# Eight rows of attention and a mixture of experts on one core: first slot reordered, two late rows' scores two a head, gathers ahead of the finishing operations

## What is computed

```python
ct_q = _lin(x, w_down_q, b_down_q)
q = (_lin(ct_q, w_up_q, b_up_q) + _rope(_lin(ct_q, wq_r, bq_r), cos, sin)).reshape(bs, sl, nh, hd)
ct_kv = _lin(x, w_down_kv, b_down_kv)
k = (k_ct + rope_k).reshape(bs, sl, nh, hd)
probs = softmax(einsum('bqhd,bkhd->bhqk', q, k) / sqrt(hd))
a = einsum('bhqk,bkhd->bqhd', probs, v).reshape(bs, sl, nh * hd)
x = x + _layernorm(_lin(a, wo, bo))
...
routed = einsum('etf,efh->eth', up * silu(gate), down_proj)   # one expert a token, times its score
shared = silu(x @ shared_gate_w) * (x @ shared_up_w) @ shared_down_w
x = x + _layernorm(shared + routed.sum(0))
```

## Time and profile before

| what | us |
|---|---|
| median of 3 timed runs (433.12 to 434.48) | 433.74 |
| the profiled execution's own time | 429.76 |
| its span, first to last instruction | 427.9 |
| TensorE busy | 397.9 (93%) |
| VectorE busy | 273.4 (64%) |
| ScalarE busy | 208.1 (49%) |
| GpSimd busy | 129.6 (30%) |
| head 0 of slot 0 on TensorE | starts at 33.48 |
| head 0 of slots 5, 6, 7 | 154.2, 178.65, 199.92 |
| last matmul ends, last VectorE instruction ends | 417.4, 425.3 |

### The profile page before, as it was taken

One profiled execution on the slowest core, in us unless ns is written; L12 is line 12 of the kernel. 1 busy time (PEld: TensorE's weight loads), 2 busy tenths in 40 slices (PEclk: granted clock), 3 DMA queues, 4 the chain that ended last, 5 costly groups with the idle time before them and its releaser, 6 DMA issues.

```text
span 427.9 us, 9422 instructions
## 1 busy us (share of the span) xinstructions
PE 397.9 (93%) x3383; PEld 299.3 (70%) x3383; DVE 273.4 (64%) x629; ACT 208.1 (49%) x383; POOL 129.6 (30%) x184
## 2 busy tenths in 40 slices
PE   7998789999999999797989999999999999999990
PEld 6675456676776767374668999999994444589990
DVE  5674478787879786877475594222225898727775
ACT  1644647676675858555561112444446766311110
POOL 1423412516253434303211101212212220026872
PEclk9999899999999999899999999999999999999997
DMA  8899326364553736460127660011111111123422
GB/s 263 204 116 122 62 70 194 87 175 136 153 156 89 216 96 209 100 199 1 52 98 230 223 215 25 26 51 51 50 51 44 44 45 35 51 59 104 141 95 86
DMA packets 50756, 47.29 MB, mean 111 GB/s; under 512 B 5334, under 2 KB 45526, under 8 KB 50710
## 3 DMA queue, kind: packets, MB, share of 16 engines
q1 hardware_dynamic: 44779, 38.31, 34.2%
q0 software_dynamic: 1632, 4.46, 3.6%
q10 hardware_dynamic: 4299, 3.92, 2.7%
HBM read 25.19 MB, written 8.65 MB: 79 GB/s over the span
## 4 chain that ended last, share of the span: by engine, by line
PE 79%; DVE 8%; DMA 4%; issue 3%; ACT 3%; POOL 2%; ACTq 0%; DVEq 0%; POOLq 0%
PE bank L1388 40%; PE bank L1707 7%; PE bank L1392 6%; PE bank L1576 6%; PE bank L1556 5%; PE bank L1517 5%; PE bank L1732 3%; DMA stacks<-mT 2%; PE bank L1455 2%; DVE nmax L1057 2%; PE bank L1445 2%; PE bank L1503 1%; DVE wall L1087 1%; DVE stats_at L991 1%; POOL rstd_at L641 1%
## 5 line engine op out<-in xcount | busy, mean ns | idle before, releaser
L1057 DVE TENSOR_REDUCE nmax<-bank 128x2 f32<-128x512 f32 x112 | 74.4, 686 | 26.4 <-PE bank L1517 25.6
L1388 PEld LDWEIGHTS bank<-stacks,wall 128*128 128x128 f32 x512 | 59.8, 192 | 2.5 <-issue 1.9
L1388 PE MATMUL bank<-stacks,wall 128*128 128x128 f32 x512 | 61.2, 276 | 0.4 <-ACT stacks L909 0.4
L1263 DVE TENSOR_TENSOR stacks<-stacks,bank 128x512 f32<-128x512 f32 x34 | 23.3, 687 | 51.7 <-PE bank L1388 49.1
L873 ACT ACTIVATE pv<-bank 128x512 f32<-128x512 f32 x64 | 38.3, 603 | 36.7 <-PE bank L1576 35.8
L1576 PE MATMUL bank<-stacks 99*128 99x256 bf16 x256 | 49.5, 276 | 3.8 <-DMA stacks<-mT 3.3
L873 ACT ACTIVATE wall<-bank 128x512 f32<-128x512 f32 x64 | 38.5, 606 | 27.2 <-PE bank L1576 26.2
L909 ACT ACTIVATE stacks<-bank 128x512 f32<-128x512 f32 x34 | 20.3, 597 | 64.3 <-PE bank L1388 54.3
L1517 PE MATMUL bank<-stacks 96*128 96x256 bf16 x224 | 43.2, 278 | 6.4 <-DVE nmax L1057 6.2
L1388 PE MATMUL bank<-wall,stacks 128*128 128x256 f32 (+1 forms) x208 | 49.2, 380 | 0.0
L706 POOL DMA_INDIRECT stacks<-x_sc,row_i x18 | 19.9, 1105 | 89.5 <-PE bank L1392 70.5
(11 more groups left out here) (207 smaller groups left out, 795.4 us busy)
## 6 DMA issues: line engine op xcount, KB each, us to landing
stacks<-low_sb SPq DMA_DIRECT2D x144, 64.0 KB, 2.5
wall<-gate_up SPq DMA_DIRECT2D x8, 1024.0 KB, 5.4
wall<-down SPq DMA_DIRECT2D x8, 512.0 KB, 6.9
y_exp<-stacks ACTq DMA_DIRECT2D x18, 128.0 KB, 1.7
x_tok<-wall SPq DMA_DIRECT2D x8, 256.0 KB, 2.5
stacks<-x_tok SPq DMA_DIRECT2D x16, 128.0 KB, 2.5
out<-stacks SPq DMA_DIRECT2D x8, 256.0 KB, 2.1
stacks<-low_sb SPq DMA_DIRECT2D x12, 128.0 KB, 5.9
```

Source lines behind the costliest of these rows:

```text
L1057: dve.tensor_reduce(nmax[:, half, qt, 2 * pair:2 * pair + 2], two(sm_bank[u % 2]), AX.X, ALU.max, negate=True).then_inc(sm["sm_max"], 1)
L1263: dve.tensor_tensor(to, sg, fu[:, :], ALU.mult).then_inc(sm["h_sb"], 1)
L1388: last = pe.matmul(out_ap, lhsT, rhs, start=(n == 0), stop=(n == len(pairs) - 1))
```

## The change

- Slot 0: unit 15 of row 0 and the down projection of row 2 come before head 0 instead of behind it. GpSimd splits the second half of the maxima of row 0 at head 0 (head 5 before), TensorE turns and ScalarE sends them at head 3 (head 5 before). The key and query copies of row 2 come at head 4, and the two query copies of row 2 move from ScalarE to VectorE (`third_q`). The units of row 1 run two a head from head 8 on (one head earlier than before), M0 of row 1 a head earlier. The first half of row 0's maxima is sent by SyncE in both versions.
- Before slot 0: 12 more matmuls of ones, and 8 each behind the first turn and the first down projection of row 0.
- Slots 5 and 6 follow a second table `late` on each engine, and `UNITS_AT` puts the units of rows 6 and 7 at one or two a head, so that the last is at head 10 and head 11. The projection `D_wo` moves from head 10 to 9, the division steps, N_v, D_aT a head earlier, the router a head earlier, M0 from head 12 or 13 to 9 and 10 (7 on GpSimd), and GpSimd splits the second half of the maxima in the same slot behind `D_power`. The turn of row 4 or 5 (`E_xn2T`) keeps its head, 3 of slot 6 and 2 of slot 7.
- First expert tiles: the turn of tile 9 (`X:9`) comes before the gate and up products of tile 8 (`GR:8`), its copy before a silu.
- Finishing operations: three pairs of gathers come before the finals, pair c + 3 after the power of final c. The first tile of pair 6 is added before the work of tile LAST - 1, into a buffer of its own, the first of pair 7 before LAST.

```diff
-WARM_ONES = 54
+WARM_ONES = 66
...
-            return w0 if (b, half) == (B - 1, 1) else w2
+            return w0 if (b, half) in ((B - 2, 0), (B - 1, 0), (B - 1, 1)) else w2
...
-        MOVED = {"A_R": 2, "A_T": 2, "A_Q": 3, "A_QK": 4, "M1": 5, "A_ev0": 5, "A_ev1": 5,
+        MOVED = {"A_R": 2, "A_T": 2, "M1": 3, "A_Q": 3, "A_QK": 4, "A_ev0": 4, "A_ev1": 4,
                  "A_khigh": 6, "A_qhigh": 7, "N_v": 8,
-                 "M0": 14}
-        AHEAD = {"B": 3, "A": 2, "N": 1, "M0": 1, "M1": 0, "C": 0, "D": -1, "E": -2}
-        PROLOGUE = ((0, "O_rows W_ones B_stats B_power B_norm B_xnT"),
+                 "M0": 13}
+        AHEAD = {"B": 3, "A": 2, "N": 1, "M0": 1, "M1": 0, "P": 0, "C": 0, "D": -1, "E": -2}
+        PROLOGUE = ((0, "O_rows W_ones B_stats B_power B_norm B_xnT W_few"),
                     (1, "B_stats B_power B_norm"),
-                    (0, "A_ones B_ct"),
+                    (0, "A_ones B_ct W_few"),
                     (1, "B_xnT"),
                     (0, "H_w A_R A_T A_Q A_kv"),
                     (2, "B_stats B_power"),
@@ -342,8 +343,9 @@
                     (1, "A_QK A_ev0"),
                     (0, "T_M0 S9 S10 S11 N_v"),
                     (1, "A_ev1 A_khigh A_qhigh A_kres A_kmid A_qres A_qmid A_klow A_qlow A_stack"),
-                    (0, "S12 S13 S14"))
-        FIRST_ROW = {0: ((2, "B_ct B_ct1"),)}
+                    (0, "S12 S13 S14"),
+                    (2, "B_ct B_ct1"),
+                    (0, "S15"))
...
+        def at_heads(*counts):
+            ends = list(accumulate(counts))
+            assert ends[-1] == NH
+            return [range(e - c, e) for c, e in zip(counts, ends)]
+        EVEN = at_heads(*[1] * NH)
+        UNITS_AT = {B - 3: at_heads(1, 1, 2, 1, 1, 1, 1, 2, 2, 2, 2),
+                    B - 2: at_heads(0, 1, 1, 1, 1, 2, 1, 1, 2, 2, 2, 2)}
         def units(b, h):
             if b:
-                return ((1, h),)
-            if h < 9:
-                return () if h else ((0, NH - 1),)
-            u = 2 * (h - 9) + (h == NH - 1)
-            return tuple((1, n) for n in range(u, u + 2 + (h >= NH - 2)))
+                heads = UNITS_AT.get(b, EVEN)
+                return tuple((1, u) for u in heads[h]) if h < len(heads) else ()
+            if h < 8:
+                return ()
+            return tuple((1, n) for n in range(2 * (h - 8), 2 * (h - 8) + 2))
...
+            if b in UNITS_AT:
+                order = late
...
+            if c >= HALF - 2:
+                return (y_first[:, 0:2, :], z_last)[c - HALF + 2]
+            return z_sb[:, p, :, :]
...
+            between.get(LAST - 1, nothing)()
             single(LAST - 1)
...
+                "P_M1_sixth": lambda b, par: m_split(b, par, 1) if b == B - 3 else None,
+                "N_M1": lambda b, par: m_split(b, par, 1),
...
-            order = {0: ("M1",), 2: ("B_power",), 8: ("A_kres", "M0",),
+            order = {0: ("P_M1",), 2: ("B_power",), 8: ("A_kres", "M0",),
...
+            late = {0: ("P_M1_sixth",), 7: ("M0",), 8: ("A_kres",), 9: ("A_qres",), 10: ("A_klow",), 11: ("A_qlow",),
+                    12: ("D_power", "N_M1"), 13: ("D_x1",), 15: ("D_power2",)}
...
-                for c in range(2):
+                for c in range(3):
...
-            after_power = {c: c + 2 for c in range(HALF - 2)}
+            after_power = {c: c + 3 for c in range(HALF - 3)}
...
+                    if b != 2:
+                        act.activation(qf[:, m, :], two(w1)[:, m, :], ACT.Identity, bias=bcol[:, 2 + m:3 + m]
+                                       ).then_inc(sm["q_sb"], 1)
...
+            late = {2: ("M1",), 3: ("E_xn2T",), 4: ("D_o1",), 5: ("A_ev0",), 6: ("A_ev1",), 7: ("A_khigh",),
+                    8: ("D_aT", "A_qhigh",), 9: ("A_kmid",), 10: ("M0", "A_qmid",), 12: ("C_o0",)}
...
-                        " s:5 y:4 s:6 w:8 y:5 s:7 y:6 x:8 w:9 y:7 s:8 x:9")
+                        " s:5 y:4 s:6 w:8 y:5 s:7 y:6 x:8 w:9 y:7 x:9 s:8")
...
+            def third_q(m):
+                def f(b, par):
+                    if b != 2:
+                        return
+                    dve.wait_ge(sm["qk_ps"], 3)
+                    dve.wait_ge(sm["ql"], 2)
+                    dve.wait_ge(sm["q_sb"], 4)
+                    dve.tensor_scalar(qf[:, m, :], two(w1)[:, m, :], bcol[:, 2 + m:3 + m], None, ALU.add
+                                      ).then_inc(sm["q_sb"], 1)
+                return f
...
+            late = {1: ("A_T", "E_xn2"), 4: ("E_router",), 5: ("D_div0",), 7: ("D_div1",), 8: ("N_v",), 10: ("D_y",),
+                    11: ("D_yn",), 13: ("D_stats",)}
...
+            def first_part(c):
+                dve.wait_ge(sm[f"gathered{c}"], 32)
+                dve.tensor_tensor(z_of(c, c % 2)[:, 0, :], y_first[:, c, :], routed[:, c, :], ALU.add
+                                  ).then_inc(sm["z_ready"], 1)
+                dve.wait_ge(sm["z_ready"], HALF + c - 1)
+                dve.bn_stats(stats_f[:, c % 2, 0, :], z_of(c, c % 2)[:, 0, :]).then_inc(sm["out_stats"], 1)
...
-                first_parts()
-            run_ffn(dve, body, final, between={LAST: between_last})
+                first_part(HALF - 1)
+            run_ffn(dve, body, final, between={LAST - 1: lambda: first_part(HALF - 2), LAST: between_last})
...
+                elif b >= B - 2:
+                    pe.wait_ge(sm["k_sb"], 2 * B)
+                    pe.wait_ge(sm["mT_sb"], 2 * b)
...
+            late = {0: ("A_R",), 1: ("A_Q",), 2: ("M1", "A_QK",), 3: ("E_xn2T",), 4: ("E_router",), 5: ("D_avT0",),
+                    7: ("D_avT1", "N_v",), 8: ("D_aT",), 9: ("M0", "D_wo",)}
...
-                        " G:6 U:6 I:0 Y:5 G:7 U:7 Y:6 X:8 Y:7 GR:8 X:9")
+                        " G:6 U:6 I:0 Y:5 G:7 U:7 Y:6 X:8 Y:7 X:9 GR:8")
```

More of the change, by code:

```diff
@@ L15 @@
 from contextlib import ExitStack
+from itertools import accumulate
 import numpy as np
@@ L383, in play, with run_slot @@
                 steps[name](int(n), int(n) % 2)
-        def run_slot(b, par, head, steps, order, last, behind):
+        def run_slot(b, par, head, steps, order, last, behind, late):
+            if b in UNITS_AT:
+                order = late
             for h in range(NH):
@@ L404, in run_slot, with run_attention @@
                 behind(b, par, h)
-        def run_attention(eng, head, steps, order, last, behind=lambda *_: None):
+        def run_attention(eng, head, steps, order, last, behind=lambda *_: None, late=None):
             for n, names in PROLOGUE:
@@ L417, in run_attention @@
             for b in range(B):
-                run_slot(b, b % 2, head, steps, order, last, behind)
+                run_slot(b, b % 2, head, steps, order, last, behind, late or order)
         def nothing(*_):
@@ L1283, in _ @@
             steps["w"] = tile_first
-            run_attention(dve, nothing, steps, order, last)
+            run_attention(dve, nothing, steps, order, last, late=late)
             play(steps, "D_div0:7 c:4 c:5 E_router:6 D_div1:7 h:0 c:6 c:7 c:8 c:9 D_y:7 h:1 D_yn:7 D_stats:7 h:2 E_xn2:7"
```

34 lines of the change are left out of this document (10 added, 24 removed).

## The result

The changed kernel took 434.51 us (431.13 to 441.11), the kernel before, run beside it, 431.79: a ratio of 1.0059, 95% interval 1.003 to 1.0088. The forecast was 433.3 with no measurable change as the likeliest class; measured was slower by 0.6%. The sum had 0.45 us less than before, and the record has 2.7 more. The range (430.1 to 436.3) held the time, but by luck: it was counted from a median before of 433.74, which rested on three runs, and from the 431.79 beside the result it would have been 428.2 to 434.4, which 434.51 just misses. Two later sets of the same changed kernel gave 0.997 and 0.9972, with intervals that end at 1.000 and 1.001. So the recorded sign is that of one set.

A forecast was written before the change was run, and what follows sets the result against it. The kernel was taken as bound by TensorE. Terms of start +0.1, slot 0 -1.3, slots 5 and 6 +1.0 and +2.8, expert part -0.45, finishing -2.6 summed to -0.45 us: median 433.3, range 430.1 to 436.3.

The forecast's parts named there:

- The sum: Whole kernel: all terms added, 0.1 - 1.3 + 1.0 + 2.8 - 0.45 - 2.6 = -0.45 us.
- head 8 could run near 43: Slot 0: maxima sent some 4.5 us earlier let head 8 start near 43 us, against 46.22 before.
- Start, +0.1: Before slot 0: 12 more matmuls of ones mostly hide in TensorE's existing wait; +0.1 us, bounds 0 and +0.5.
- Slot 0, -1.3: Slot 0: row 1's first unit starts at 46.2, slot 1 at 60.2, not 61.48; -1.3 us, bounds -2.5 and 0.
- The other bound: Slot 0: row 1's first unit needs the stack's last transfer, issued about 37.6, 8.3 us to land, so about 46.
- Slots 5 and 6, +3.8: Late order of slots 5 and 6: slot 5 costs +1.0 us and slot 6 +2.8 us, delay reaching the end.
- The local waits for maxima: Slots 5 and 6, up to the projection: TensorE waits for VectorE's maxima, 1.5 and 1.25 us; bounds 0 and 2.
- Expert part, -0.45: First expert tiles: with `X:9` ahead of `GR:8`, the 0.47 us wait for its copy is covered; -0.45 us.
- Finishing, -2.6: Finishing operations: VectorE's 2.22 us gather wait goes and pair 6's first tile moves ahead; -2.6 us, bounds -2.9 and -1.8.
- it ends at 415.1: Finishing: pair 6's first tile delays the last hidden product, which still ends before TensorE needs it at 415.6; otherwise 0.8 us returns.
- Rival C: Slots 6 and 7: the longer wait ahead of `E_xn2T` drops TensorE's clock behind it; +2.1 us, 435.8; chance 0.27.
- Rival B: Slots 5 and 6: the pairs cost no local waits, slots give -0.5 and +1.6; sum -3.15, 430.6; chance 0.30.

The follow-up runs named there:

- slot0_only: The kernel before with the new prologue and slot 0 alone (54 matmuls of ones): 0.9962 of the kernel before.
- second trace: Profile of another execution of the changed kernel, unaltered, span 426.3 us; its timed set took 0.9970 of the kernel before.
- best1: Changed kernel with slots 5 and 6 as before, 54 ones, no groups of 8, pair 5's sums in their own buffer: 0.9864 of the kernel before.
- changed_third: The changed kernel, unaltered, run as a third set: 0.9972 of the kernel before.
- no_slot0: The changed kernel with the prologue and slot 0 in the order of before: 1.0034 of the kernel before.
- filled: The changed kernel with 36 matmuls of ones in slot 7, in TensorE's wait ahead of the turn of row 5: 0.9940 of the kernel before.
- no_late: The changed kernel with slots 5 and 6 back in the order of before: 0.9872 of the kernel before.
- stack_pause: Changed kernel, SyncE sending the middle and low parts of row 1's stack only after row 0's second half of maxima landed: 435.23 us, run once.

## Why the prediction was right or wrong

The change was to take 0.45 us off and put 2.7 on. From the trace of before to the recorded one the sum is missed by 2.4 us, and two steps of the text failed: in slot 0 that head 8 could run near 43 (1.3 us), and at the end that VectorE's work on pair 6 stays covered and nothing else waits (2.1 us); slots 5 to 7 came out 0.75 us cheaper than forecast. 0.7 us of the record's 2.7 is the two executions at the lowest clocks, without which the median is 433.78. The later sets miss the sum by under 1 us, with the same steps wrong.

**Start, +0.1.** Held within its bounds in most traces: seven of fourteen with 66 ones start as before, the rest 0.3 to 1.0 us later. The recorded execution had 0.49, the upper bound.

**Slot 0, -1.3.** The size held (slot0_only -1.6; the second trace -0.77, with the ones in it). The step that failed is "head 8 could run near 43": it priced the maxima's DMA at about the 3.2 us that it took before, while its issue had been moved into the time in which row 1's stack fills every DMA engine; it took up to 7.7. In the trace of before too it had ended beside the stack's landing (46.08), so an earlier issue alone promised nothing. The other bound, the stack's landing, was named and is what ends the wait. But the stack lands anywhere from 44.7 to 47.6 in the traces with this slot 0 (48.55 in best1, which starts late), and 8.3 us of one row was taken as fixed. Slot 1 so begins between 57.9 (changed_third: stack at 44.7, no fall of the clock) and 62.9, in the record at 61.56 against the forecast 60.2. That the gain still came out near 1.3 in slot0_only is partly luck.

**Slots 5 and 6, +3.8.** Held, the best step: +3.05 against before, +3.25 against slot0_only (64.73), all with the same two falls, the chain to the turn within 0.1 us at each station, one wait of 2.27 us where the text put it. In its own terms, slot 5 up to the turn of row 4 was sized at 1.0 and measured 0.7 (28.31 us against 27.62), and from there to the turn of row 5 2.8 and 2.6 (23.17 against 20.59). The local waits for maxima are 0.8 us in each slot and not 1.5 and 1.25, and 1.5 and 1.1 us of waiting for ScalarE's exponential stand in their place. Where no fall lies ahead of the turn of row 4, slot 5 costs 1.3 to 1.5 (28.1 to 28.3 in four traces against 26.8 in four): the fall hides a part of the cost, the wait for the low parts of the stack among it. changed_third, no_slot0 and filled, with one fall in slot 6, have 69.3 to 69.5 for slots 5 to 7, and six traces without the late order, with one fall, 64.7 to 65.6. In timed runs the late order costs 4.2.

**Expert part, -0.45.** The wait is gone in every trace with `X:9` first. Not foreseen: 1.15 us at 394 in the recorded execution, cause open.

**Finishing, -2.6.** Held without the waits (-2.9). The step that fell in the recorded execution is the cover "it ends at 415.1": the lower bound of the gain, -1.8, allowed for 0.8 us of TensorE's waiting, and it was 0.99. The cause was named wrongly. Not pair 6's first tile alone, but VectorE's wait for the store of pair 3 ahead of pair 5's sum, 1.32 us, and that sum's second addition beside GpSimd's, 1.34 us longer than otherwise; the rows of before show neither.

**The sum and the class.** The two traces give +1.9 and -1.6, the sum said -0.45; the three sets give +0.6, -0.3 and -0.3%. The sum was right to within what single executions scatter. What the record added, in its own trace and against the second: 0.85 us up to slot 1 from a later start (0.35) and a later stack, 1.15 at 394 and 0.99 at the end. Why the first set as a whole stands 0.9% above the later ones is open: the executions behind its ratio had a mean clock of 0.981, against 0.985 and 0.988, which at 0.3 us for each 0.001 is 1 to 2 us of the 3.8.

**Rival C** (0.27; 435.8) is the nearest to the record in number: executions at a lower clock reach 441 us. But they lift the median by only 0.7 us, and a fall behind the turn, which is what the rival says, is in no trace. The Trainium skill (TensorE: Matmul & The Clock Gate, section "HAM oscillation — how this bites in real kernels") has waits between bursts send the clock down; the counts and slot 0 lean to it, while slot 7 has eight waits of about 2 us with no fall behind them. **Rival B** fell: 0.8 us of local waits in each slot and the long one are there.

**What the sum hid.** The text's own terms without slots 5 and 6 are 0.1 - 1.3 - 0.45 - 2.6 = -4.25 us; no_late measured -5.5. The faster version stood in the working.

## What to carry to other kernels

When a sum of several edits comes out near zero, run the edits with a gain without the one with the loss: no_late beats both kernels by 1.0 to 1.3%. Removing two waits of 0.8 and 1.1 us by bringing work forward pays only if that work isn't in the chain that the next wait stands for; follow that chain station by station, as here it could be forecast to a tenth of a microsecond. Before moving a small DMA earlier, look at what the DMA engines carry at the new time, and at what landed last at the old one: its old latency belongs to the old place. And compare stretches of two traces only where the clock falls at the same places; here a fall in slot 5 hid 0.6 to 0.8 us of the new order's cost.

## What the runs showed of the hardware

- A 12 KB transfer of ScalarE's queue took at most 2.25 us with the DMA engines idle (stack_pause) and up to 7.7 us issued into 128 KB transfers of SyncE's (changed): none of its 27 packets ran for 5.5 us, while over 670 others did, and head 8, which waits for its landing, started 1.4 us behind its last packet.
- The stack's last transfer, issued at 38.0 to 38.6 us, landed between 44.7 us (changed_third) and 47.6 us (no_late) in different executions of the same code.
- TensorE's clock fell in stretches of 3.4 or 6.8 us, one to three of them in a trace ahead of the end; the changed kernel's executions had mean clocks from 0.963 to 0.993, and each 0.001 went with 0.3 us.
- An addition of VectorE on 128x256 took 0.41 us alone and 1.5 to 2.1 us beside GpSimd's addition on 128x512 (second addition of pair 5, ten traces).
- Waits of VectorE and SyncE on one TensorE product ended together, 3.4 to 3.5 us long, in three traces, each time at 393 to 395 us, with six to eight gathers just issued.
